# A graph layer's node steps: x + beta split over two engines, the comparison in eight pieces, a shorter root

## What is computed

```
h = relu(_layernorm(x))
edge_input = concat([h[src], h[dst], edge_attr, coord[src], coord[dst]])
messages   = silu(edge_input @ mW1 + mb1) @ mW2 + mb2
aggregated = segment_sum(messages, dst)
u   = silu(concat([h, aggregated, coord]) @ uW1 + ub1)
upd = u @ uW2 + ub2
out = x + _layernorm(h + upd, gamma, beta)
```

## Time and profile before

| | us |
|---|---|
| median of 3 runs | 720.5 |
| lowest and highest of them | 715.4 and 722.17 |
| the profiled execution, its own time | 722.67 |
| its span, first to last instruction | 720.8 |

### The profile page before, as it was taken

One profiled execution on the slowest core, in us unless ns is written; L12 is line 12 of the kernel. 1 busy time (PEld: TensorE's weight loads), 2 busy tenths in 40 slices (PEclk: granted clock), 3 DMA queues, 4 the chain that ended last, 5 costly groups with the idle time before them and its releaser, 6 DMA issues.

```text
span 720.8 us, 17511 instructions
## 1 busy us (share of the span) xinstructions
PE 630.0 (87%) x3830; PEld 466.2 (65%) x3830; DVE 642.1 (89%) x3060; ACT 516.5 (72%) x1034; POOL 541.0 (75%) x448
## 2 busy tenths in 40 slices
PE   1468999999999999999998998998998998999981
PEld 0235676766776776766766766766767767767771
DVE  4365699999999999999999999999999999999897
ACT  1546778778877787787787787787788788788630
POOL 7778878888888888888888888888888888881210
PEclk9966999999999999999999999999999999999997
DMA  6445556666666666666765766756666766765231
GB/s 133 111 115 131 151 164 160 186 187 163 180 186 163 190 179 163 189 181 161 194 177 160 204 169 166 202 163 170 199 160 179 196 156 180 198 161 173 87 122 69
DMA packets 119053, 118.54 MB, mean 164 GB/s; under 512 B 48764, under 2 KB 93615, under 8 KB 119010
## 3 DMA queue, kind: packets, MB, share of 16 engines
q1 hardware_dynamic: 104884, 91.41, 43.6%
q0 software_dynamic: 12608, 26.25, 16.4%
q10 hardware_dynamic: 1518, 0.42, 0.3%
HBM read 79.31 MB, written 38.70 MB: 164 GB/s over the span
## 4 chain that ended last, share of the span: by engine, by line
POOL 60%; issue 21%; PE 8%; DVE 6%; ACT 2%; DMA 1%; POOLq 1%; ACTq 0%
POOL ends_in L373 47%; POOL x_beta L393 13%; ACT ends_norm L532 2%; DVE y_out L749 1%; DVE centred L632 1%; PE ps_e L458 1%; PE ps_t L486 1%; PE ps_hid L445 1%; PE ps_hid L447 1%; PE ps_e L457 1%; PE ps_e L456 1%; DVE stats L677 1%; PE ps_t L464 1%; DMA ends_in<-in_rows,end_idx 1%; PE ps_f L490 0%
## 5 line engine op out<-in xcount | busy, mean ns | idle before, releaser
L373 POOL DMA_INDIRECT ends_in<-in_rows,end_idx x392 | 422.6, 1078 | 113.3 <-issue 112.5
L476 PE MATMUL ps_upd<-w_out,hidden_n 128*128 128x128 f32 x784 | 140.4, 284 | 33.6 <-DVE centred L632 31.6
L532 ACT ACTIVATE ends_norm<-ends_in,minus,rstd 128x128 f32<-128x128 f32 x392 | 155.9, 484 | 6.6 <-DVE minus L743 6.6
L532 ACT ACTIVATE x_norm<-x_in,minus,rstd 128x128 f32<-128x128 f32 x392 | 156.0, 488 | 6.3 <-DVE minus L743 6.3
L476 PEld LDWEIGHTS ps_upd<-w_out,hidden_n 128*128 128x128 f32 x784 | 119.4, 192 | 41.9 <-DVE centred L632 26.4
L393 POOL TENSOR_TENSOR x_beta<-x_in,beta_row 128x1024 f32<-128x1024 f32 x49 | 116.0, 2368 | 39.1 <-DVE y_out L749 38.2
L632 DVE SCALAR_TENSOR_TENSOR centred<-ps_upd,y_mean,gamma_row 128x128 f32<-128x128 f32 x392 | 135.0, 347 | 0.1
L447 PEld LDWEIGHTS ps_hid<-match,msg_in 113*128 113x128 f32 x784 | 103.0, 191 | 47.2 <-issue 47.2
L537 ACT ACTIVATE ends_t<-ps_t 128x1024 f32<-128x1024 f32 x49 | 50.2, 1024 | 90.9 <-PE ps_f L490 89.3
L477 PE MATMUL ps_upd<-const_sb,h_t 128*128 128x128 f32 x392 | 107.6, 274 | 0.0
L749 DVE SCALAR_TENSOR_TENSOR y_out<-centred,rstd,x_beta 128x128 f32<-128x128 f32 x392 | 107.1, 348 | 0.0
(11 more groups left out here) (79 smaller groups left out, 885.7 us busy)
## 6 DMA issues: line engine op xcount, KB each, us to landing
x_in<-in_x_steps SPq DMA_DIRECT2D x49, 512.0 KB, 5.2
out<-y_out SPq DMA_DIRECT2D x49, 512.0 KB
msg_in<-msgs SPq DMA_DIRECT2D x392, 56.4 KB
msgs<-msg SPq DMA_DIRECT2D x49, 258.0 KB
ends_in<-in_rows,end_idx POOLq DMA_INDIRECT x392
ends_in<-in_attr SPq DMA_DIRECT2D x49, 64.0 KB
end_idx<-in_ends SPq DMA_DIRECT2D x49, 4.0 KB
match<-in_node_vec SPq DMA_DIRECT2D x49, 4.0 KB
```

Of the source, the lines that this page charges most:

```text
L373: nc.gpsimd.indirect_dma_start(out=dst, out_offset=None, in_=rows, in_offset=bass.IndirectOffsetOnAxis(ap=end_idx[s.slot][:, t, side:side ...
L476: nc.tensor.matmul(ps_upd[:, cols(j)], hidden_n[:, cols(j)], w_out[:, :], start=j % E_TILES == 0, stop=False)
L532: return nc.scalar.activation(dst, source, function, bias=minus[was][:, c:c + 1], scale=rstd[was][:, c:c + 1])
```

## The change

It has four parts. (1) `x_beta` is made by two engines: GpSimd adds tiles 0 to 4 (128 x 640), VectorE tiles 5 to 7 (128 x 384, `add_beta`, between `rstd` and `minus`). (2) The comparison becomes eight `tensor_scalar` operations of one tile each, 112 x 128: to a constant row of positions `iota` the first row operand (the number of the block's first node) is added, and the result is compared with the second row operand (the message's destination). `place` and its semaphore go, and the comparison moves behind `minus`. `iota` now counts from 0 to 1023 and is loaded by a DMA of its own on GpSimd's queue, ahead of the first gathers. (3) The root's constants are scaled so that one operation fewer does: `root_d` goes, and `root_c` becomes a `scalar_tensor_tensor`. (4) The destination indices are copied into `msg` by ScalarE, between `hidden_e` and `h_t`, and no longer by VectorE.

```
+POOL_TILES = 5
...
-                    nc.gpsimd.tensor_tensor(x_beta[near.slot][:, :, :], x_in[near.slot][:, :, :],
-                                            beta_row[:, :, :].broadcast_to([P, N_TILES, H]), ALU.add).then_inc(x_beta_ready, 1)
+                    nc.gpsimd.tensor_tensor(x_beta[near.slot][:, 0:POOL_TILES, :], x_in[near.slot][:, 0:POOL_TILES, :],
+                                            beta_row[:, :, :].broadcast_to([P, POOL_TILES, H]), ALU.add).then_inc(x_beta_low_ready, 1)
...
+            pool.dma_start(iota[:, :, :].rearrange("p j m -> p (j m)"), iota_row.rearrange("(o n) -> o n", o=1).broadcast_to([P, N_STEP])).then_inc(iota_loaded, 16)
...
+                if own:
+                    act.wait_ge(edge_loaded[own.slot], (own.fills4 + 1) * 16)
+                    wait(act, msg_stored[own.slot], 16 * own.fills4)
+                    nc.scalar.activation(msg[own.slot][:, :, H:H + 1], end_idx[own.slot][:, :, 1:2], ACT.Copy).then_inc(dst_copied, 1)
...
-                    V.tensor_tensor(place[near.half][0:WINDOW, :, :], msg_in[near.half][0:WINDOW, :, H:H + 1],
-                                    base, ALU.subtract).then_inc(place_ready, 1)
...
-                    V.tensor_tensor(match[near.half][0:WINDOW, :, :], place[near.half][0:WINDOW, :, :].broadcast_to([WINDOW, N_TILES, P]),
-                                    iota[0:WINDOW, :, :].broadcast_to([WINDOW, N_TILES, P]), ALU.is_equal).then_inc(match_ready, 1)
+                    for j in range(N_TILES):
+                        last = V.tensor_scalar(match[near.half][0:WINDOW, j, :], iota[0:WINDOW, j, :],
+                                               const[0:WINDOW, bass.ds(C_BASE + N_TILES * near.n, 1)],
+                                               msg_in[near.half][0:WINDOW, j, H:H + 1], ALU.add, ALU.is_equal)
+                    last.then_inc(match_ready, 1)
...
+                    V.tensor_tensor(x_beta[near.slot][:, POOL_TILES:, :], x_in[near.slot][:, POOL_TILES:, :],
+                                    beta_row[:, :, :].broadcast_to([P, N_TILES - POOL_TILES, H]), ALU.add).then_inc(x_beta_high_ready, 1)
...
-                V.tensor_scalar(root_c[:, at], root_b[:, at], 0.375, -1.25, ALU.mult, ALU.add).then_inc(stat_ops, 1)
+                V.scalar_tensor_tensor(root_c[:, at], root_b[:, at], 10.0 / 3.0, root_b[:, at], ALU.subtract, ALU.mult).then_inc(stat_ops, 1)
...
-                V.tensor_tensor(root_d[:, at], root_c[:, at], root_b[:, at], ALU.mult).then_inc(stat_ops, 1)
...
-                V.scalar_tensor_tensor(halley[:, at], root_d[:, at], 1.875, guess[:, at], ALU.add, ALU.mult).then_inc(stat_ops, 1)
+                V.scalar_tensor_tensor(halley[:, at], root_c[:, at], 5.0, guess[:, at], ALU.add, ALU.mult).then_inc(stat_ops, 1)
```

More of the change, by code:

```diff
@@ L46 @@
 MAGIC = 0x5F3759DF
-C_IDENT, C_LOWER, C_IOTA = 0, P, 2 * P
-C_BOUND = 3 * P
+C_IDENT, C_LOWER = 0, P
+C_BOUND = 2 * P
 C_SEARCH = C_BOUND + PER_LANE + 1
@@ L143, in gnn_layer @@
 def gnn_layer(nc, rows, x_steps, ends, dst_all, dst_seen, attr, node_vec, mW1, mb1, mW2, mb2, uW1, ub1, uW2, ub2,
-              gamma, beta, consts, out):
+              gamma, beta, consts, iota_row, out):
     f32, bf16, i32 = mybir.dt.float32, mybir.dt.bfloat16, mybir.dt.int32
@@ L203, in gnn_layer @@
         msg_in = [sb(f"msg_in{b}", [P, N_TILES, MSG_ROW]) for b in range(2)]
-        place = [sb(f"place{b}", [P, N_TILES, 1]) for b in range(2)]
+        iota = sb("iota_sb", [P, N_TILES, P])
         match = [sb(f"match{b}", [P, N_TILES, P]) for b in range(2)]
@@ L213, in gnn_layer @@
         y_mean = sb("y_mean", [P, N_TILES])
-        guess, halley, root_a, root_b, root_c, root_d, newton_a, newton_b = (
-            sb(n, [P, NS]) for n in ("guess", "halley", "root_a", "root_b", "root_c", "root_d", "newton_a", "newton_b"))
+        guess, halley, root_a, root_b, root_c, newton_a, newton_b = (
+            sb(n, [P, NS]) for n in ("guess", "halley", "root_a", "root_b", "root_c", "newton_a", "newton_b"))
         rstd = [sb(f"rstd{b}", [P, NS]) for b in range(RING)]
@@ L567, in _ @@
             run_steps(act, body)
-        STAT_OPS = 12
+        STAT_OPS = 11
         HALF = N_TILES // 2
@@ L644, in evict_messages, with match_nodes @@
                                     fold_bias[:, :, :].broadcast_to([P, E_TILES, H]), ALU.add).then_inc(msg_ready, 1)
-                def copy_dst():
-                    if not own:
-                        return
-                    dve.wait_ge(edge_loaded[own.slot], (own.fills4 + 1) * 16)
-                    wait(dve, msg_stored[own.slot], 16 * own.fills4)
-                    V.tensor_copy(msg[own.slot][:, :, H:H + 1], end_idx[own.slot][:, :, 1:2]).then_inc(dst_copied, 1)
-                def place_messages():
+                def match_nodes():
                     if not near:
@@ L688, in body @@
                 if not (new or nxt or prev):
-                    copy_dst()
                     evict_messages()
-                    place_messages()
+                    add_beta()
                     match_nodes()
@@ L733, in body @@
                 evict_messages()
                 dve.wait_ge(stat_ops, base + 11)
-                V.scalar_tensor_tensor(newton_b[:, at], newton_a[:, at], -0.5, var[:, at], ALU.mult, ALU.mult).then_inc(stat_ops, 1)
-                place_messages()
-                dve.wait_ge(stat_ops, base + 12)
                 wait(dve, ends_norm_ready, it.edges_upto(-RING))
                 wait(dve, x_norm_ready, it.nodes_upto(-2))
-                V.scalar_tensor_tensor(rstd[b][:, at], newton_b[:, at], 1.5, halley[:, at], ALU.add, ALU.mult).then_inc(rstd_ready, 1)
@@ L741, in body @@
-                match_nodes()
+                V.scalar_tensor_tensor(rstd[b][:, at], newton_b[:, at], 1.5 * 0.375, halley[:, at], ALU.add, ALU.mult).then_inc(rstd_ready, 1)
+                add_beta()
                 dve.wait_ge(rstd_ready, 2 * it.stats_before() + 1)
                 V.scalar_tensor_tensor(minus[b][:, at], s_add[:, at], -0.5, rstd[b][:, at], ALU.mult, ALU.mult).then_inc(rstd_ready, 1)
+                match_nodes()
                 if prev:
                     dve.wait_ge(centred_ready, 2 * prev.n + 2)
-                    dve.wait_ge(x_beta_ready, prev.n + 1)
+                    dve.wait_ge(x_beta_low_ready, prev.n + 1)
+                    dve.wait_ge(x_beta_high_ready, prev.n + 1)
```

25 lines of the change are left out of this document (14 added, 11 removed).

## The result

The changed kernel takes 754.32 us (median of 4 runs, 751.54 to 756.8); the kernel before takes 720.1 beside it (715.4 to 722.17). The ratio is 1.0484, 95% interval 1.0419 to 1.0548: slower by 5%, and above the predicted range of 708 to 750. The profiled execution has a span of 754.8 us, 34.0 more than before.

What follows compares the result with a forecast made beforehand. GpSimd was taken to bound the kernel at 13.45 us an iteration. From 722.67 us, 43 x (13.36 - 13.45) = -3.9, + 0.6 + 2.4 = -0.9 gives 721.8; forecast 721.5 us, range 708 to 750.

Steps and rivals of the forecast that it cites:

- Who is bound: GpSimd, bound at 13.45 us an iteration, gains 0.89 as x_beta falls to 1.49; VectorE becomes the bound at 13.26, 13.36 with lock.
- p: Time of one of VectorE's eight comparisons: forecast 0.19 us, from a one-source copy's 0.13 plus 0.06 for both row operands.
- The sum with it: VectorE's work per iteration, 11.74 us plus eight comparisons; forecast 13.26 us, plus 0.1 for waits on GpSimd's lock.
- GpSimd's 13.45: The period in us of the kernel before, read from its x_beta starts and taken as GpSimd's.
- The rival that said so: Row operands of VectorE's comparison fetched one after the other: 0.25 us each, 744 us; chance 0.30 together with the single rate.
- Ends: Outside the full iterations: +0.6 us for one more DMA ahead of the first gathers, +2.4 for four last VectorE node steps.
- Edits at nothing: VectorE's destination copy gains 0; ScalarE's copy costs 0, going into its 0.42 us wait for the transposes ahead of h_t.
- the 0.2 that was allowed for: TensorE's wait for the comparison ahead of hid: forecast 0; over 0.2 us would show the forecast wrong.
- The free-operand rival: Row operands cost nothing in VectorE's comparison: 0.13 us each, the TensorE and ScalarE ring ends last, 708.5 us; chance 0.17.
- The long-lock rival: Comparisons and y_out on VectorE hold off GpSimd's gathers as one, up to 3.6 us: 776 us; chance 0.08.

Runs made afterwards that it cites:

- run 2: The changed kernel with 111 one-column memsets ahead of VectorE's loop, nothing within the loop changed: 740.76 us, ratio 1.0279.
- run 6: The changed kernel with place and one broadcast comparison instead of the eight, still behind minus and directly ahead of y_out: 752.39 us, ratio 1.046.
- run 5: The kernel before with 24 probe comparisons ahead of the pipeline, with none, one or two row operands: steps of 0.34, 0.40 and 0.46 us at 512 columns.
- run 3: The changed kernel with constants in place of both row operands of the eight comparisons: 738.59 us.
- run 7: The changed kernel with constants for both row operands and 111 memsets ahead of VectorE's loop: 739.21 us, ratio 1.0231.

## Why the prediction was wrong

- **Who is bound.** Right: GpSimd was relieved (`x_beta` 1.54 us, forecast 1.49) and VectorE took its place.
- **p, "the copy, at its double rate, with 0.06 for both row operands fetched together".** This step failed first. The double rate and the 0.06 were right; together was wrong. Each is fetched by itself: 0.136 + 2 x 0.063 = 0.26. The sum with it is 11.74 + 2.1 = 13.84, measured 13.74 without pauses. By the prediction's own terms VectorE passes GpSimd's 13.45 at p = (13.45 - 0.1 - 11.74) / 8 = 0.20, not at 0.21, so the forecast stood 0.01 from the edge. The rival that said so gave 744 us, and the same kernel with its code moved takes 740.8. Its chance should have been the larger one, since `y_out` and `centred` both showed a row operand's price and no row showed two for one.
- **A term that was missing.** Nowhere did the prediction ask how long VectorE's loop code had become and where it lay. The pauses at the loop's turn cost 13.6 us and carried the time out of the range. By the median: 720.1, + 591.5 - 578.0 = 13.5 for the 43 periods of run 2, + 4.5 at its two ends, + 13.6 for the pauses, is 751.7; measured 754.3.
- **Ends.** Forecast +0.6 and +2.4, measured +2.8 and +2.2. The DMA of `iota` (0.55 us) moved the first gather by 0.31 only, from 3.44 to 3.75; the other 2.5 us of the start were not looked into.
- **Edits at nothing, and the small ones.** The destination copy on ScalarE takes 0.20 us and leaves 0.32 of `h_t`'s wait: no cost, no gain, as said. `add_beta` 0.47 and `root_d` 0.09 as said.
- **TensorE.** It does wait for the comparison, 16.3 us in all, 0.33 a step, beyond the 0.2 that was allowed for; that fits the larger p, and the chain puts the period on VectorE (72%), not on TensorE (8%).
- **The free-operand rival**, which the Trainium skill's page "VectorE: DVE Perf Modes" (the TRN2 errata) supported with 0.127 us for such an operation: the runs give 0.136 with constants, close to it, but 0.26 with two row operands, for which the page has no term. The measurement decides.
- **The long-lock rival** had a lock that the runs show, but not in this kernel. The Trainium skill's page "SBUF — State Buffer" (Who interferes with whom) counts one-source operations in a two-port mode and operations with two SBUF inputs among those that lock GpSimd out. The whole comparison, with two inputs, does as it says (run 6). The form with constants does so in part: 4 of 12 gathers that start in it are held. The form with row operands keeps the double rate (run 5) and holds none of 44, against the rule as the prediction applied it. Why is not shown.

## What to carry to other kernels

Price an operation by its form, operands included: eight pieces with two row operands each cost more than one broadcast operation, 2.1 us against 1.15. Where two engines hold each other off, look at what stands back to back: the comparison ahead of `minus` and not behind it, and `add_beta` well ahead of both, were worth 36 us here. A small link between two long operations is no guarantee, so count the held gathers after each move. And when a change makes a loop's program longer, look at the instruction queue's packets: if they rise with the turns of the loop, pad the code and measure again before judging the change.

## What the runs showed of the hardware that was not expected

- A row operand of a one-source VectorE operation costs 0.063 us, each by itself, at 128 and at 512 columns, and leaves the double rate alone: steps of 0.34, 0.40 and 0.46 us at 512 columns with none, one and two.
- Without row operands a chain of such operations can hold off a gather of GpSimd: 4 of 12 that start in it (3.67 to 3.73 us, run 3), and 13 of 39 that start in the two-source operation ahead of it (up to 4.45 us, run 7). With one or two row operands it held none (0.94 to 1.06 us).
- A hold can run on across instructions of different lines that follow back to back: `add_beta`, `minus`, `match` and `y_out` as one, 4.38 us, in 12 of 40 cases (run 6).
- Fifteen instructions more in the loop (341 to 356) and eleven more ahead of it brought 8 pauses of 0.8 to 3.3 us; 111 memsets outside the loop took them away.
- An engine can be relieved and the period stay: with all of `x_beta` on GpSimd, VectorE's small operations grew by 0.58 us, where the removed work had cost 0.47.
